# A one-core transformer block: three transfers moved forward in SyncE's order, and one wait of ScalarE relaxed

## What is computed

```
x = x + layernorm(attention(layernorm(x)))
x = x + layernorm(ffn(layernorm(x)))

attention: q, k, v = x Wq, x Wk, x Wv
           scores = q^T k / 4         (512 x 512: over features, summed over tokens)
           out    = (softmax(scores) v^T)^T Wo
ffn:       inter = silu(x gate^T) * (x up^T)
           out   = inter down^T
```

## Time and profile before

| | |
|---|---|
| three runs, median (lowest to highest) | 719.9 us (717.62 to 720.74) |
| the profiled execution's own time | 722.85 us |
| its span, first to last instruction | 721.0 us |
| mean granted TensorE clock | 0.972 of full speed |
| busy: PE, DVE, POOL, ACT | 93%, 68%, 61%, 52% |
| DMA traffic | 115 MB, 159 GB/s over the span |

### The profile page before, as it was taken

How to read it: one execution, slowest core, us unless ns; L and a number is a source line. 1 busy time by engine, 2 the same in 40 slices (tenths; PEclk the granted TensorE clock), 3 DMA queues, 4 the chain that set the end, 5 groups by cost and what they waited for, 6 DMA issues and landing times. The chain is left out here.

```text
span 721.0 us, 16306 instructions
## 1 busy us (share of the span) xinstructions
PE 667.9 (93%) x5872; PEld 468.7 (65%) x5872; DVE 491.9 (68%) x977; ACT 373.6 (52%) x651; POOL 440.1 (61%) x615
## 2 busy tenths in 40 slices
PE   5898899999999999999977689999999999999896
PEld 3686686878778786877863346565665656665464
DVE  7657964479635885366577677877878788865542
ACT  3532332333323332333347567778777787777642
POOL 6098958628585576970245456667666666666542
PEclk9898999999999999999998799999999999999999
DMA  6835447415482246830299564657475757646222
GB/s 216 327 99 177 152 162 257 151 30 174 167 263 85 90 146 190 282 103 16 66 248 282 124 171 119 175 163 191 149 193 160 190 147 188 155 132 183 79 78 98
DMA packets 65549, 114.98 MB, mean 159 GB/s; under 512 B 12624, under 2 KB 29136, under 8 KB 65488
## 3 DMA queue, kind: packets, MB, share of 16 engines
q1 hardware_dynamic: 65488, 114.16, 53.8%
HBM read 81.76 MB, written 32.37 MB: 158 GB/s over the span
## 5 line engine op out<-in xcount | busy, mean ns | idle before, releaser
L1420 POOL TENSOR_TENSOR act<-inter,act 128x512 f16<-128x512 f32 x128 | 157.9, 1240 | 93.4 <-ACT act L1460 93.3
L1464 ACT ACTIVATE gated<-gbank,c_gate 128x512 f32<-128x512 f32 x128 | 87.4, 683 | 56.9 <-PE gbank L1622 56.9
L1537 DVE SCALAR_TENSOR_TENSOR inter<-ubank,c_up,gated 128x512 f32<-128x512 f32 x128 | 95.8, 748 | 28.4 <-ACT gated L1464 24.2
L1664 PE MATMUL ybank<-down,act 128*128 128x160 f16 x512 | 109.8, 234 | 0.0
L1666 PE MATMUL ybank<-down,act 128*128 128x160 f16 x512 | 109.1, 233 | 0.0
L1665 PE MATMUL ybank<-down,act 128*128 128x160 f16 x512 | 109.1, 233 | 0.0
L1460 ACT CAST act<-inter 128x512 f16<-128x512 f32 x128 | 78.0, 609 | 4.2 <-DVE inter L1537 4.2
L1664 PEld LDWEIGHTS ybank<-down,act 128*128 128x128 f16 x512 | 50.0, 98 | 29.5 <-issue 25.7
L1622 PE MATMUL ubank<-z,s_all 128*32 128x512 f16 x512 | 52.4, 399 | 17.9 <-DVE inter L1537 16.6
L1622 PE MATMUL gbank<-z,s_all 128*32 128x512 f16 x512 | 52.9, 403 | 5.6 <-DMA z<-token_features 3.8
L687 DVE SCALAR_TENSOR_TENSOR tu_lo<-chain,tu_hi 128x512 fp32r<-128x512 f32 x32 | 22.1, 691 | 45.0 <-ACT tu_hi L555 44.9
(11 more groups left out here) (196 smaller groups left out, 1911.4 us busy)
## 6 DMA issues: line engine op xcount, KB each, us to landing
x_ln<-x SPq DMA_DIRECT2D x64, 256.0 KB, 3.5
z<-token_features SPq DMA_DIRECT2D x64, 256.0 KB, 5.1
job<-job_in SPq DMA_DIRECT2D x24, 640.0 KB, 4.1
shared<-x SPq DMA_DIRECT2D x32, 256.0 KB, 2.8
x<-shared SPq DMA_DIRECT2D x32, 256.0 KB, 2.0
token_features<-z_hi SPq DMA_DIRECT2D x32, 256.0 KB, 3.8
x_res<-x SPq DMA_DIRECT2D x32, 256.0 KB, 2.9
out<-x_res SPq DMA_DIRECT2D x32, 256.0 KB, 3.0
```

The lines of the kernel that those rows point to most:

```text
L1420: pool.tensor_tensor(hidden[par][:, i, TOK:2 * TOK], inter[:, i % INTERS, :], hidden[par][:, i, 0:TOK], ALU.subtract).then_inc(inter_ready, 1)
L1464: act.activation(gated[:, slot % 2, :], gbank[:], ACT.Silu, scale=c_gate[:]).then_inc(silu_done, 1)
L1537: dve.scalar_tensor_tensor(out=inter[:, i % INTERS, :], in0=ubank[:], scalar=c_up[:], in1=gated[:, i % 2, :], op0=ALU.mult, op1=ALU.mult). ...
L1664: pe.matmul(out, hidden[par][:, r, high], box[:, 0], start=False, stop=False)
```

## The change

- ScalarE waits for `wov_done` 1 instead of 2 before the exponentials.
- In the last batch, z half 0 of group 0 is loaded at t = 2 instead of t = 4: behind the load of x_ln 6, ahead of the stores of tiles 3 and 4 and of residuals 6 and 7.
- The twelve down weight transfers, with the waits around them, become `jobs()` and are called in quad 0 of group 0, behind the load of x_ln 8.
- In quad 2 the load of z half 1 moves behind the store of output 1 and the reload. In quad 1 the order stays as it was.

```diff
-                    if not more and t == 4:
+                    if not more and t == 2:
                         sp.wait_ge(chain_done, b * CHAIN + 3 * K)
                         ffn_in.load_z(sp, feats, 0, 0, 0)
...
-                act.wait_ge(wov_done, 2)
+                act.wait_ge(wov_done, 1)
                 if not more:
                     feats.high(act, 0)
...
-            def regroup(g, par, half, loads_before):
-                spread(g, par, half, loads_before)
-                ffn_in.load_z(sp, feats, g, par, half)
...
+            def jobs():
+                attention.jobs_stored(sp)
+                for b in range(I // PER):
+                    sp.dma_start(w_box[:, b * PER:(b + 1) * PER], d_dram[b][:, 0:PER]).then_inc(ffn_in.down_loaded, 16)
+                    for c in range(2):
+                        bank, quarter = (2 * b + c) // 4, (2 * b + c) % 4
+                        sp.dma_start(w_mom[:, bank, :, quarter * P:(quarter + 1) * P], d_dram[b][:, PER + c, :, 0:P]
+                                     ).then_inc(ffn_in.down_loaded, 16)
+                attention.all_stored(sp)
...
             def quad(g, par, count, j, made, begun, more):
                 for ahead in ((0,), (1, 2, 3), (), ())[j] if more else ():
                     m = g * Q + ahead + AHEAD + 2
                     sp.wait_ge(feats.h_normed, m - RING + 1)
                     feats.load(sp, x1_t, m, (ahead + AHEAD + 2) % RING)
+                if isinstance(g, int) and g == 0 and j == 0:
+                    jobs()
                 last = isinstance(g, int) and g == GROUPS - 1
                 if j == 2 and not last:
-                    regroup(g + 1, 1 - par, 1, count)
+                    spread(g + 1, 1 - par, 1, count)
...
                 if j == 1 and not last:
                     if isinstance(g, int) and g == 0:
                         spread(g + 1, 1 - par, 0, count)
-                    ffn_in.load_z(sp, feats, g + 1, 1 - par, 0)
+                if j in (1, 2) and not last:
+                    ffn_in.load_z(sp, feats, g + 1, 1 - par, j - 1)
...
             for q in range(2):
                 load_res(0, q)
-            attention.jobs_stored(sp)
-            for b in range(I // PER):
-                sp.dma_start(w_box[:, b * PER:(b + 1) * PER], ...
-                for c in range(2):
-                    sp.dma_start(w_mom[:, bank, :, quarter * P:(quarter + 1) * P], ...
-            attention.all_stored(sp)
             schedule(sp, quad)
```

More of the change, by code:

```diff
@@ L1396, in _ @@
                 load_res(0, q)
-            attention.jobs_stored(sp)
-            for b in range(I // PER):
-                sp.dma_start(w_box[:, b * PER:(b + 1) * PER], d_dram[b][:, 0:PER]).then_inc(ffn_in.down_loaded, 16)
-                for c in range(2):
-                    bank, quarter = (2 * b + c) // 4, (2 * b + c) % 4
-                    sp.dma_start(w_mom[:, bank, :, quarter * P:(quarter + 1) * P], d_dram[b][:, PER + c, :, 0:P]
-                                 ).then_inc(ffn_in.down_loaded, 16)
-            attention.all_stored(sp)
             schedule(sp, quad)
```

## The result

| | before | after |
|---|---|---|
| median of 20 runs each, us | 720.49 (717.62 to 724.32) | 716.61 (713.97 to 722.39) |
| profiled execution, us (its span) | 722.85 (721.0) | 713.97 (712.2) |

The ratio is 0.994, with a 95% interval of 0.9923 to 0.9958: 4.3 us of 720.5 gained, 3.0 to 5.5. The forecast was 7.6 us of gain and 712.3; the time lies inside the range of 708.5 to 717.0, near its slow end. A little over half of the forecast gain came.

A forecast was written before the change was run, and what follows sets the result against it. TensorE, busy 93% of the span, was taken as the bound, so only its standstills counted. Gains of 1.0 + 1.2 + 3.7 + 1.7 = 7.6 us from the 719.9 median gave 712.3, range 708.5 to 717.0.

The forecast's parts named there:

- part 2: Start of token groups: z half 0 loaded ahead of two stores ends TensorE's wait; -1.2 us, bounds -1.2 and +3.7.
- main forecast: Whole kernel: the four gains arrive about as summed, a gain of 5 to 9.5 us; chance 0.62.
- rival B: 380 to 400 us: busy DMA queue makes ninth tile or residuals late; 715.2, up to 718.9; chance 0.19.
- the far end: Last batch: residual 7 up to 3.7 us late for VectorE at 8.3 us per landing; 717.2 in all.
- The sign named for a wrong part 2 or 3: A DMA wait on VectorE between 372 and 400 us would show the forecast wrong there.
- Part 3: First token group: ninth x tile loaded ahead of twelve weight transfers ends VectorE's wait; -3.7 us, bounds -2.0 and -4.2.
- part 4: Last groups, quad 2: store and reload ahead of z's second half end VectorE's residual wait; -1.7 us, bounds 0 and -2.4.
- Rival C: Groups 1 to 6: z's second half slips, TensorE waits at step 6; slower, 726.1 at 11 us slip; chance 0.03.
- Part 1: Batch 0: exponentials wait for one half of the split weights; -1.0 us, bounds 0 and -4.4.
- GpSimd's wait that should have held the gain to 0.99: Batch 0: GpSimd idles 0.99 us at 65.54, so at most 0.99 of 1.30 us comes through.
- the 2 that I had named as too much: Batch 0: TensorE passing 89 over 2 us earlier would show the exponentials' forecast wrong.
- A, the clock: TensorE's low clock goes with the waits, gaining more than the sum; 708.9; chance 0.10.

The follow-up runs named there:

- only_z: Kernel before with only z half 0 of the last batch loaded at t = 2 instead of t = 4: 723.75 us against 721.36, ratio 1.0043.
- z_at_2_res6: Kernel before with only z half 0 at t = 2, the load of residual 6 put ahead of it: 722.71 us against 719.55, ratio 1.0058.
- whole_but_z: Whole change except that z half 0 stays at t = 4, against the kernel before: 714.76 us against 721.44, ratio 0.9903.
- best_guess: Whole change but with z half 0 at t = 3 instead of t = 2, against the kernel before: 713.54 us against 721.44, ratio 0.988.
- z3_tile9: Kernel before with z half 0 at t = 3 and x_ln 8 loaded ahead of the twelve weight transfers: 714.38 us against 719.55, ratio 0.9938.
- only_tile9: Kernel before with only the load of x_ln 8 ahead of the twelve weight transfers: 719.42 us against 721.36, ratio 0.9977.
- whole_again: The whole change timed once more against the kernel before, on another set's chip: 716.08 us against 721.44, ratio 0.9934.

## Why the prediction was right and wrong

**Direction and range: right.** The time fell clear of what a measurement can tell from no change, and inside the range. The size was 3.3 us too large, and by the timed runs nearly all of that is one term: without part 2 the change gave 7.0 us, where the other three terms add up to 6.4. The gain of 4.3 us lies below the 5 to 9.5 of the main forecast, on the ground of rival B.

**Part 2, the step that failed.** The step took residual 7 at the fast landing (6.4 us twice), found it in time for VectorE, and so kept only the gain, -1.2. It measured +3.1 alone, and +2.2 inside the whole by the two ratios. That +3.1 lies within the stated -1.2 to +3.7 is luck: the far end was worked out from a late residual 7, and no trace shows VectorE wait for that. The sign named for a wrong part 2 or 3, a DMA wait of VectorE between 372 and 400, did come, for residual 6. The gain itself is real: the stage from the last batch to the Silu is 1.5 us shorter in all seven kernels with an earlier z. Two things were left out.

- *The queue, not the consumer.* The landings were not the mistake. The first leg, tile 3's store, was put at 6.4 us and took 6.6 in the profile after, 7.0 in only_z and 7.4 in z_at_2_res6, against 3.4 in the kernel before and in z_at_3, where it stands ahead of z. The second leg, residual 7's load, was put at 6.4 too and took 2.7 to 3.0, so the residual was in time. But its load waits on SyncE for the store's landing, and that holds SyncE for 5.2 to 6.4 us, where in the kernel before it waited 2.1 for VectorE. The loads and stores behind are held with it. I had asked when the residual is wanted, and not what else stands behind it on SyncE.
- *Residual 6.* Its load also stands behind z. It takes 6.7 us to land instead of 3.5, and VectorE wants it 4.4 us after its issue (366.87 to 371.30 in the profile after). VectorE waits 2.39 us, TensorE 2.29 in turn. The prediction named this load among those pushed back and gave it no time at all. The wait appears in three of the four kernels with z at t = 2 (the fourth, z_at_2_res6, has the load ahead of z) and in none with z at t = 3 or t = 4.

The timed runs show that the order costs: z ahead of tile 3's store is +3.1 and +4.2, z behind it +0.2. The path from there to the time is shown for a smaller part only. By the stages of the last section part 2 alone gives -1.5 + 2.3 = +0.8. Where the other 2.3 us (3.4 in z_at_2_res6) come from stays open; the profiles of both kernels are also longer in a stage ahead of the place, which is told under what stays open. Inside the whole, the two profiles with part 2 have spans of 712.2 and 712.8 us and that of whole_but_z 713.0: they don't show the cost at all, both having been taken on runs below their medians (by 2.6 and 1.5 us). Inside the whole the cost stands on the timed runs alone.

The Trainium skill, DMA: Bandwidth & Descriptors, section "Queues, rings and completion order", has a completion signal land only after every earlier write of its engine. The store's landing after 6.6 to 7.4 us behind z, against 3.4 without z ahead of it, agrees with it. By that rule the prediction said that the sum would lean to the far end of this term, and then went by the row of the z loads instead. The direction was right, but residual 7, on which that far end was reckoned, was not late.

**Part 3, right in the mechanism; its size by the stages, not by the timed run.** The ninth tile's wait is gone in all eight kernels with this part, and the stage is 3.6 us shorter over fourteen profiles. The timed run of this part alone gave only 1.7 (0.7 to 2.7), which is what a rival to it had said beforehand, on the ground that the stall in the profile of before was unusually long. That ground does not hold: the stage is 20.92 us there, against a mean of 21.0 over the six kernels without this part. In its profile the wait at the end of the kernel, the one of part 4, cost 11.95 instead of 10.33, with the granted clock at 0.64 behind it. That is one profile, and whether it holds for the median isn't shown, so the gap between 3.6 and 1.7 stays open.

**Part 4, right.** The interval with the stall is 10.33 or more in all eight kernels without this part and 8.65 in all six with it; the timed run gave 1.9. Rival C did not happen: TensorE has no wait for z at a group's step 6 in the profile after. Its only wait for z there, 0.43 us at 411.08, is for half 0 of group 1, where the kernel before waits 0.60.

**Part 1, right as far as it can be seen.** 1.4 us by the stages, 0.8 by the timed run, whose interval takes in zero. The first exponential at 46.29 came a microsecond sooner than forecast, and GpSimd's wait that should have held the gain to 0.99 was replaced by one of 1.52 us for a job's transfer at 65.30. TensorE passed the point at 89 by 2.04 us earlier, a hair past the 2 that I had named as too much; but the profile of before is itself some 2 us slow in this stage (179.2 against a mean of 177.1). Nearer to the place, at the first output of batch 0, the mean is 93.2 us over the eight kernels without the part and 92.1 over the six with it: 1.1 us, close to the forecast.

**Rivals.** B is what came in number, at 716.6 where it gave 715.2 to 718.9. In its mechanism it was half right: a residual behind z's half 0 came late, but the ninth tile, of which it said the same, lands in time. A, the clock: the mean granted clock of the two profiles rose from 0.972 to 0.984, and the gain still stayed below the sum; low stretches remain, such as 0.63 from 384 to 388 us in the profile after.

**What stays open.** In five of the seven profiles with z at t = 2 or 3 the granted clock falls once between 320 and 328 us, ahead of anything that the moved loads touch; it does in none of the other seven. By stretch, in the profile of after, in that of only_z, and then in that of whole_but_z:

```profile
320.00:324.00 4.00, 3.82 (x15) 2.64 (x16) 2.69 (x6) 1.05 (x2) 0.00 (x0) 0.57 0.00 0
```

```profile
324.00:328.00 4.00, 4.00 (x16) 3.30 (x16) 2.07 (x5) 0.60 (x1) 0.74 (x2) 0.50 0.00 0
```

```profile
320.00:324.00 4.00, 3.58 (x21) 2.51 (x21) 3.41 (x6) 0.63 (x2) 0.00 (x0) 1.00 0.00 0
```

The stage from the first output of batch 1 to that of batch 3 takes 177.8 to 179.9 us in the five (179.7 in only_z, 179.9 in z_at_2_res6) and 176.7 to 177.6 in the other nine. That is as large as what is missing in part 2's account, but nothing connects the two. The instructions and their order are the same there in all fourteen, so chance isn't excluded; if the spell belongs to the earlier z, best_guess pays it too. No run here takes it apart. Nor is it settled whether z at t = 3 is better than at t = 4 once part 3 is there (0.988 against 0.9903, intervals overlapping); z3_tile9 against only_tile9 says so by intervals that just miss each other, but on different chips.

## What to carry to other kernels

When a bulk load is moved ahead in a queue, don't ask only whether each load behind it still comes in time. Look for the first instruction behind it that waits for a landing, since that one holds the whole issuing queue, and ask what the hold delays. Look also for what is wanted soonest among the loads that now stand behind. Here the move by two steps of the loop cost 3 us alone, and the move by one step, which stays behind the store that the next load waits for, cost nothing that could be measured (+0.2). The stages at the place account for about a quarter of the 3 us, so such a price is to be measured and not only added up.

A stall that is hidden by a later stall of the same chain is worth nothing until that one is gone. So parts are to be tried together with what bounds behind them: z's earlier start gave nothing alone and, with the ninth tile early, probably a gain (-4.5 against -1.7, on different chips).

## What the runs showed that I had not expected

- A 256 KB store that landed in 3.4 us took 6.6 to 7.4 behind four loads of 256 KB, on the same queue.
- One wait of 2.57 us on TensorE was followed by 12 us at half clock (380 to 392 in only_z), and one of 2.45 in whole_again likewise (376 to 388). The one of 2.29 in the profile after was not: 0.77 from 376 to 380, then 0.80. The prediction had counted such a stretch once, behind the wait at 400.
- Two profiles differed by 8.9 us where the medians differed by 3.9. On a kernel of 720 us whose runs spread over 7, only stage lengths over several profiles could be set against a sum of terms of 1 to 4 us.
